# Differential attention on one Trainium2 core: the short tile's row maximum as one reduction and one small scaling

## The chip, the cores and the metric

The kernel runs on one core of a Trainium2 chip. The metric is the device time of one launch in microseconds (us), the median of several runs. A core has a matrix engine (TensorE, PE in the rows, with its weight loads as PEld), a vector engine (VectorE, DVE), an activation engine (ScalarE, ACT), a general engine (GpSimd, POOL) and SyncE (SP), which here issues the transfers. Each has its own instruction stream, and they order one another with semaphores. SBUF is the memory on the chip, PSUM the one into which TensorE writes.

## The reference

The input is x of 8 x 512 x 512 in float32. The output is a chain of three residual blocks, each on a layer-normalised x:

```python
x = x + 0.5 * ffn(layernorm(x))     # expert choice over 16 experts, one shared expert matrix
x = x + attn(layernorm(x))          # differential attention
x = x + 0.5 * ffn(layernorm(x))
```

The attention has 16 heads of width 32 with two maps each and 4 key/value heads. What the change touches is the first softmax, over energies that are masked causally:

```python
energy = where(causal, NEG, einsum("bqhad,bkhad->bahqk", qd, kd))
scores = softmax(energy / sqrt(D), axis=-1)          # a = 0, 1: two maps
diff   = softmax(where(causal, NEG, scores[:, 0] - lam * scores[:, 1]), axis=-1)
att    = einsum("bhqv,bvhd->bqhd", diff, v)          # then an RMS norm per head and @ Wo
```

## The kernel before, in words

The program has three stages: the first FFN, the attention with the first half of the second FFN, and the selection of experts and the last sum. The change lies in the second, from about 350 to 1725 us of the profile.

That stage is a software pipeline. 4096 rows are 32 tiles of 128. A body (`run_bodies`) works on three tiles at once: the attention of tile group K, the preparation of a later tile (layer norm, QKV product, rotary embedding, transposes) and the closing of an earlier one (head norm, output product, residual, second layer norm, router and expert product). Each body has 8 steps j of 3 slots. A step is one pair of query tiles of one head, chosen so that the work is the same in each: `tiles(j)` is (0, 3) for even j and (1, 2) for odd j, a short tile of 1 or 2 key blocks of 128 and a long one of 4 or 3. With two maps the short tile has 2 x 128 or 2 x 256 columns, the long one 2 x 512 or 2 x 384.

All engines run the same 24 slots in the same order, written out by hand in their own lists, each with lags in steps. In one step, for the pair in work:

- TensorE (`energies`, L1559 and L1561) makes the energies of the long tile and then the short one in PSUM and adds the mask.
- VectorE (`row_bias`, L1134) takes one instruction per tile and map: it multiplies the energies in PSUM in place by minus the scale (`nesc`) and accumulates their minimum in `nbias`. An accumulating instruction shows as two in the trace, the main one and a `READ_ACCUMULATOR`.
- ScalarE (`exps`, L1415) computes exp(-1 * value + nbias) from PSUM into `ex`, and accumulates the row sum in `esum`. For the short tile it waits for all four bias values of the step.
- VectorE one step later takes reciprocals (`inv_sums`, L1141) and the factor `gam` (`gamma`, L1148). GpSimd masks (`mask`, L1307) and scales the second map (`scale`, L1314). VectorE subtracts the maps and accumulates the maximum (`difference`, L1160) and makes `dbias` (L1169). GpSimd (`shift`, L1321) and ScalarE (L1424) apply the second softmax's bias, TensorE transposes (`turn_diff`, L1573), ScalarE takes the exponential (`probs`, L1432), and TensorE multiplies by the values (`weigh`, L1591).

Around the attention, in the same order: VectorE's rotary products (L1224, L1233), which GpSimd adds (L1346) and splits (L1361); VectorE's layer-norm statistics (L1195 to L1199); its head sums (L1243 to L1250), from which GpSimd takes a power (`head_root`, L1390); VectorE's head norm (`head_norm`, L1256), whose result goes over ScalarE (L1469) and GpSimd (`low_heads`, L1367) to a transpose on TensorE (L1605); and GpSimd's further work on tiles of 512 columns (`low`, L1352; `square`, L1384). Each engine works in order, so what waits holds up all behind it.

Of the kernel before, what the change touches and what calls it, by code (L numbers as in the profile page):

```python
# [15 lines left out]
ALU = mybir.AluOpType  # L16
# [4 lines left out]
I32 = mybir.dt.int32  # L21
X = mybir.AxisListType.X
# [3 lines left out]
P = 128  # L26
# [38 lines left out]
SC_E, SC_R, SC_Q, SC_O = range(4)  # L65
# [79 lines left out]
def run_bodies(eng, attention, side, ahead, alone, spread, closing):  # L145

    def body(K, tau, pi, pairs=True, more=True):
        known = {}
        for j in range(STEPS):
            for i in range(3):
                for lag, f in attention[i] if pairs else ():  # L160
                    back = j < lag
                    if not isinstance(K, int) or 0 <= K - back < NT:
                        f(Place(known, K, back, (j - lag) % STEPS, j - lag))
                for f in side.get(3 * j + i, ()):
                    f(tau, pi)
                for f in ahead.get(3 * j + i, ()):
                    if tau is not None and more:
                        f(tau + 1)

    for slot in sorted(ahead):  # L170
        for f in ahead[slot]:
            f(0)
    spread[0] = True
    with eng.Fori(0, AHEAD) as tau:
        for f, next_tile in alone:
            f(tau + 1 if next_tile else tau)
    spread[0] = False
    body(0, AHEAD, None)
    with eng.Fori(1, BEHIND) as K:
        body(K, K + AHEAD, None)  # L180
    with eng.Fori(BEHIND, NT - AHEAD - 1) as K:
        body(K, K + AHEAD, K - BEHIND)
    body(NT - AHEAD - 1, NT - 1, NT - 1 - AHEAD - BEHIND, more=False)
    with eng.Fori(NT - AHEAD, NT) as K:
        body(K, None, K - BEHIND)
    body(NT, None, NT - BEHIND)
    spread[1] = True
    for f, next_tile in closing:
        if next_tile:
            f(NT - BEHIND + 1)  # L190
    with eng.Fori(NT - BEHIND + 1, NT - 1) as pi:
        for f, next_tile in closing:
            f(pi + 1 if next_tile else pi)
    for f, next_tile in closing:
        if not next_tile:
            f(NT - 1)
    spread[1] = False


def program(nc, x, wqkv, wo, we, wr, lams, rms, rb, eb, consts, out, x1_d, x2_d, y2_d):  # L200
    top = ExitStack()

    def maker(ctx):
        def sb(name, shape, dt=F32):
            return ctx.enter_context(nc.sbuf_tensor(name, shape, dt))

        def ps(name, shape, dt=F32):
            return ctx.enter_context(nc.psum_tensor(name, shape, dt))

        def sem(name):  # L210
            return ctx.enter_context(nc.semaphore(name))

        return sb, ps, sem

    with top:
# [10 lines left out]
        esc = sb("esc", [P, 4])  # L226
        nesc = sb("nesc", [P, 1])
# [216 lines left out]
        with ExitStack() as ctx:  # L444
# [12 lines left out]
            part = sb1("part", [P, 2, KT])  # L457
# [16 lines left out]
            def spare(first, tiles):  # L474
# [18 lines left out]
            consts_done, bn_done, mv_done, ve_done, nm_done = (sem1(n) for n in (  # L493
                "consts_done", "bn_done", "mv_done", "ve_done", "nm_done"))
            rstd_done, xn_done, xt_done, hi_done, lo_done = (sem1(n) for n in (
                "rstd_done", "a_xn_done", "a_xt_done", "a_hi_done", "a_lo_done"))
# [40 lines left out]
            def _(sp):  # L537
# [30 lines left out]
                for i in range(PIECES):  # L568
                    if i >= 2:
                        sp.wait_ge(piece_lo, i - 1)  # L570
                    source, raw, _, _, _ = piece(i)
                    sp.dma_start(raw, source).then_inc(piece_in[i % 2], 16)
# [352 lines left out]
        with ExitStack() as ctx:  # L925
            sb2, ps2, sem2 = maker(ctx)
# [21 lines left out]
            pr = [sb2(f"pr{i}", [P, PAIR]) for i in range(2)]  # L948

            nbias = sb2("nbias", [P, 8, 2, 2])  # L950
            esum = sb2("esum", [P, 8, 2, 2])
            rsum = sb2("rsum", [P, 8, 2, 2])
            gam = sb2("gam", [P, 8, 2])
# [5 lines left out]
            at = sb2("at", [P, 2, E], F16)  # L959
# [19 lines left out]
            def sig(name, credit=CREDIT):  # L979
                return Signal(sem2(name), credit)  # L980


            x_in, st_done, ve_done, rstd_done, xn_done = sem2("x_in"), sig("st_done"), sig("ve_done"), sig(
                "rstd_done"), sig("xn_done")
            hi_done, lo_done, xt_done, xt_out = sig("hi_done"), sig("lo_done"), sig("xt_done"), sig("xt_out")
            rhi_done, rlo_done = sig("rhi_done"), sig("rlo_done")
            proj_done, rope_v, rope_done, v_done = sig("proj_done"), sig("rope_v"), sig("rope_done"), sig("v_done")
# [2 lines left out]
            ones_set = sem2("ones_set")  # L990

            e_done, bias_done, exp_done = sig("e_done"), sig("bias_done"), sig("exp_done")
            rs_done, gam_done, masked, scaled = sig("rs_done"), sig("gam_done"), sig("masked"), sig("scaled")
            diff_done, dbias_done = sig("diff_done"), sig("dbias_done")
            shifted_short, shifted_long = sig("shifted_short"), sig("shifted_long")
            dt_done, prob_done, av_done, att_out = sig("dt_done"), sig("prob_done"), sig("av_done", 64), sig("att_out")
# [5 lines left out]
            xr_in, st2_done, ve2_done, rstd2_done, xn2_done = sem2("xr_in"), sig("st2_done"), sig("ve2_done"), sig(  # L1002
                "rstd2_done"), sig("xn2_done")
# [25 lines left out]
            def tiles(j):  # L1029

                return ((0, 3), (1, 2))[j % 2]

            def span(j, i):

                first = P * (tiles(j)[0] + 1)
                return (0, first) if i == 0 else (first, PAIR)

            def energy(j, i):


                n = P * (tiles(j)[i] + 1)
                short, long = ((2, slice(0, 2)), (1, slice(0, 4, 3)), (0, slice(2, 4)), (3, slice(1, 3)))[j % 4]
                if i == 0:
                    return bank[:, short, 0:2 * n].rearrange("p (a n) -> p a n", a=2)
                return bank[:, long, 0:n]
# [73 lines left out]

            @blk.vector  # L1120
            def _(dve):
                for s in (st_done, ve_done, xn_done, st2_done, ve2_done, xn2_done, rope_v, bias_done, rs_done, gam_done, diff_done, dbias_done, att_out,
                          ss_done, s2_done, de_done, an_done, x2_done, lg_out):
                    s.start(dve)
                dve.memset(vs[:, :, :, D:DV], 1.0).then_inc(ones_set, 1)


                def row_bias(i):
                    def f(at):
                        j = at.j  # L1130
                        e_done.wait(dve, at.units(2, 1 - i))
                        for a in range(2):
                            part = energy(j, i)[:, a, :]
                            dve.tensor_scalar(part, part, nesc[:, 0:1], None, ALU.mult, ALU.min,  # L1134
                                              accum_out=nbias[:, j, i, a:a + 1]).then_inc(bias_done.sem, 1)
                    return f

                def inv_sums(at):
                    j = at.j
# [12 lines left out]
                def difference(i):  # L1152

                    def f(at):
                        j = at.j
                        if i == 0:
                            scaled.wait(dve, at.units(2, 1))
                            dt_done.wait(dve, at.units(2, 1 - 8), apart_v)
                        lo, hi = span(j, i)
                        dve.tensor_tensor_reduce(out=df[j % 4][:, lo:hi], in0=ex[j % 4][:, 0, lo:hi],  # L1160
                                                 in1=ex[j % 4][:, 1, lo:hi], scale=1.0, scalar=-3e38,
                                                 op0=ALU.subtract, op1=ALU.max, accum_out=dmax[:, j, i:i + 1])\
                           .then_inc(diff_done.sem, 1)
                    return f
# [115 lines left out]
                def take_logits(u):  # L1280
# [2 lines left out]
                       .then_inc(lg_out.sem, 1)  # L1283

                run_bodies(dve,
                           [[(0, row_bias(1)), (0, row_bias(0))],
                            [(1, inv_sums), (1, gamma), (4, diff_bias), (3, difference(0))],
                            [(8, take_head), (3, difference(1))]],
                           {2: [post(head_sums)], 4: [post(head_norm)], 5: [rope(0)], 9: [rope(1)], 11: [post(add)],
# [113 lines left out]
            def _(ac):  # L1403
                for s in (hi_done, xt_out, rhi_done, v_done, turned_out, exp_done, shifted_long, prob_done, ah_done, at_out, hi2_done,
                          xt2_out, y_out):
                    s.start(ac)
                ac.wait_ge(ones_set, 1)

                def exps(i):
                    def f(at):  # L1410
                        j = at.j
                        lo, hi = span(j, i)
                        for a in range(2):
                            bias_done.wait(ac, at.units(4, a if i == 1 else 3))
                            ac.activation(ex[j % 4][:, a, lo:hi], energy(j, i)[:, a, :], ACT.Exp,  # L1415
                                          bias=nbias[:, j, i, a:a + 1], scale=-1.0,
                                          accum_out=esum[:, j, i, a:a + 1]).then_inc(exp_done.sem, 1)
                    return f

# [373 lines left out]
```

## Time and profile before

| | |
|---|---|
| median of 3 runs | 1957.39 us (1941.44 to 1961.42) |
| profiled execution | 1944.41 us, of which the span is 1942.3 us |
| PE, DVE, ACT, POOL busy, share of the span | 77%, 75%, 65%, 56% |
| mean granted TensorE clock | 0.848 of full speed |
| `exps`, ACT L1415 | 1024 instructions, 527.7 us busy |
| `row_bias`, DVE L1134 | 1024 instructions, 503.6 us busy |

How to read it: a busy time is the sum over an engine's instructions, and on VectorE an instruction's record can overlap the next one's, so the distance from start to start tells what an instruction costs its engine. An instruction that the engine has taken up and that waits for a memory port counts as busy. The 1942.3 us hold three stages with different limits; the rows below are mostly of the middle stage.

### The profile page before, as it was taken

Reading aid. Unit: us, or ns where it says so; the run is one execution under the profiler, and the core shown is the slowest. Engines: PE = TensorE matmul, PEld = TensorE weight load, DVE = VectorE, ACT = ScalarE, POOL = GpSimd, SP = SyncE. Lnnn points to the kernel's source line nnn. Section 1 sums busy time; section 2 is a strip of 40 time slices with the busy share of each in tenths; the row PEclk is TensorE's granted clock in tenths of the full one; section 3 lists DMA queues with packets and bytes.
Section 4 is the critical chain, followed back from the end, with each engine's and each line's share of the span. In section 5 each row is a group of like instructions: output and inputs, shape, how many; then the busy total and the mean of one; then the engine's idle time right before and its main releaser. Section 6 shows DMA issues by size and latency. Waiting matters only on the chain. (4 is left out here: it accounts for less than half of the span.)

```text
span 1942.3 us, 44349 instructions
## 1 busy us (share of the span) xinstructions
PE 1497.7 (77%) x10688; PEld 1038.7 (53%) x10688; DVE 1449.4 (75%) x5497; ACT 1258.2 (65%) x3422; POOL 1097.1 (56%) x1505
## 2 busy tenths in 40 slices
PE   3995434588888888998889988998889888885520
PEld 3542211366666666666666666666666666663210
DVE  6687211687889889898898889898898867751268
ACT  2361121687878888888888888887888877852120
POOL 5320222565677777677776777677777655652200
PEclk9997767688889989899999989899999778766655
DMA  7025111111111111121111111121111100001176
GB/s 288 3 81 184 31 35 42 26 38 33 28 32 54 42 42 47 46 53 45 44 53 42 47 42 47 46 53 44 44 53 41 40 16 22 16 17 33 38 268 259
DMA packets 179669, 117.25 MB, mean 60 GB/s; under 512 B 139169, under 2 KB 139553, under 8 KB 179618
## 3 DMA queue, kind: packets, MB, share of 16 engines
q1 hardware_dynamic: 179618, 116.65, 20.4%
q8 instruction: 22, 0.36, 0.1%
q14 instruction: 29, 0.24, 0.0%
HBM read 51.57 MB, written 33.55 MB: 44 GB/s over the span
## 5 line engine op out<-in xcount | busy, mean ns | idle before, releaser
L1415 ACT ACTIVATE ex<-bank,nbias 128x512 f32<-128x512 f32 (+3 forms) x1024 | 527.7, 538 | 67.5 <-DVE bank L1134 64.8
L1134 DVE TENSOR_SCALAR_CACHE_REDUCE bank<-bank,nesc 128x512 f32<-128x512 f32 (+3 forms) x1024 | 503.6, 553 | 61.9 <-PE bank L1561 60.8
L1591 PEld LDWEIGHTS bank<-vs,pr 128*128 128x128 f32 x2560 | 334.6, 206 | 23.2 <-issue 12.2
L1591 PE MATMUL bank<-vs,pr 128*128 (+1 forms) x2560 | 339.7, 284 | 8.6 <-issue 4.1
L1573 PE MATMUL bank<-cst,df 128*128 128x128 f32 x1280 | 264.5, 309 | 86.7 <-ACT pr L1432 85.9
L1314 POOL TENSOR_SCALAR ex<-ex,gam 128x128 f32<-128x128 f32 (+3 forms) x512 | 314.0, 624 | 0.0
L1559 PE MATMUL bank<-ks,qs 96*128 (+2 forms) x1024 | 262.1, 333 | 50.9 <-ACT ex L1415 48.7
L1432 ACT ACTIVATE pr<-bank 128x128 f32<-128x128 f32 (+3 forms) x512 | 231.7, 453 | 88.8 <-PE bank L1573 87.7
L1160 DVE CUSTOM_DVE_ANT_0 df<-ex 128x128 f32<-128x128 f32 (+3 forms) x512 | 258.9, 520 | 8.8 <-issue 4.5
L1573 PEld LDWEIGHTS bank<-cst,df 128*128 128x128 f32 x1280 | 168.0, 165 | 114.2 <-ACT pr L1432 98.3
L1415 ACT ACTIVATION_READ_ACCUMULATOR ex<-bank,nbias 128x1 f32 x1024 | 222.8, 218 | 0.0
L1561 PE MATMUL bank<-mask_b,ident_b 128*128 128x128 bf16 x1024 | 207.7, 237 | 0.0
L1424 ACT ACTIVATE df<-df,dbias,rsum 128x512 f32<-128x512 f32 (+1 forms) x256 | 201.6, 787 | 0.0
L1559 PEld LDWEIGHTS bank<-ks,qs 96*128 (+1 forms) x1024 | 109.7, 107 | 140.9 <-issue 73.3
L1346 POOL TENSOR_TENSOR rot<-rot,scratch 128x512 f32<-128x512 f32 (+1 forms) x96 | 105.1, 1095 | 123.8 <-DVE scratch L1233 123.8
L1321 POOL TENSOR_SCALAR df<-df,rsum,dbias 128x128 f32<-128x128 f32 (+1 forms) x256 | 149.9, 586 | 39.4 <-DVE dbias L1169 39.3
L1361 POOL TENSOR_TENSOR split<-rot,split 128x512 f16<-128x512 f32 (+1 forms) x96 | 95.3, 992 | 123.5 <-ACT split L1460 123.5
L247 PE MATMUL bank<-wqkv_h,b_xt 128*128 128x512 f16 (+1 forms) x384 | 156.2, 407 | 8.0 <-ACT b_xt L1484 5.9
L248 PE MATMUL bank<-wqkv_l,b_xt 128*128 128x512 f16 (+1 forms) x384 | 156.1, 406 | 0.0
L249 PE MATMUL bank<-wqkv_h,b_xt 128*128 128x512 f16 (+1 forms) x384 | 155.7, 406 | 0.0
L1134 DVE DVE_READ_ACCUMULATOR bank<-bank,nesc 128x1 f32 x1024 | 142.9, 140 | 0.0
L1148 DVE SCALAR_TENSOR_TENSOR gam<-esum,lam,rsum 128x2 f32<-128x2 f32 x256 | 115.2, 450 | 33.8 <-DVE rsum L1141 24.9
(279 smaller groups left out, 2958.5 us busy)
## 6 DMA issues: line engine op xcount, KB each, us to landing
qs<-turned SPq DMA_DIRECT2D x384, 64.0 KB, 2.1
x_dram<-xa SPq DMA_DIRECT2D x8, 1024.0 KB, 4.9
b_xs<-x_dram SPq DMA_DIRECT2D x32, 256.0 KB, 2.6
x<-x_dram SPq DMA_DIRECT2D x32, 256.0 KB, 2.6
x_dram<-x SPq DMA_DIRECT2D x32, 256.0 KB, 2.0
y_dram<-scratch SPq DMA_DIRECT2D x32, 256.0 KB, 2.0
c_x<-x_dram SPq DMA_DIRECT2D x8, 1024.0 KB, 14.5
c_y<-y_dram SPq DMA_DIRECT2D x8, 1024.0 KB, 15.0
```

The lines of the kernel that those rows point to most:

```text
L247: eng.matmul(acc, a_hi(k), b_hi(k), start=first and k == 0, stop=False)
L248: eng.matmul(acc, a_hi(k), b_lo(k), start=False, stop=False)
L1134: dve.tensor_scalar(part, part, nesc[:, 0:1], None, ALU.mult, ALU.min, accum_out=nbias[:, j, i, a:a + 1]).then_inc(bias_done.sem, 1)
L1160: dve.tensor_tensor_reduce(out=df[j % 4][:, lo:hi], in0=ex[j % 4][:, 0, lo:hi], in1=ex[j % 4][:, 1, lo:hi], scale=1.0, scalar=-3e38, op0=A ...
L1314: gp.tensor_scalar(ex[j % 4][:, 1, lo:hi], ex[j % 4][:, 1, lo:hi], gam[:, j, i:i + 1], 1.0, ALU.mult, ALU.mult).then_inc(scaled.sem, 1)
L1415: ac.activation(ex[j % 4][:, a, lo:hi], energy(j, i)[:, a, :], ACT.Exp, bias=nbias[:, j, i, a:a + 1], scale=-1.0, accum_out=esum[:, j, i, ...
L1424: ac.activation(df[j % 4][:, lo:hi], df[j % 4][:, lo:hi], ACT.Identity, bias=dbias[:, j, 1:2], scale=rsum[:, j, 1, 0:1]).then_inc(shifted_ ...
L1432: ac.activation(pr[j % 2][:, lo:hi], bank[:, 6, 0:hi - lo], ACT.Exp).then_inc(prob_done.sem, 1)
L1559: pe.matmul(out_e, q.rearrange("p a n -> p (a n)"), k.rearrange("p a n -> p (a n)"), start=True, stop=True)
L1561: mm = pe.matmul(out_e[:, n - P:n], ident_b[:, :], mask_b[:, :], start=False, stop=True, skip_group_check=True)
L1573: tr = pe.transpose(bank[:, 6, k * P:(k + 1) * P], df[j % 4][:, lo + k * P:lo + (k + 1) * P], ident)
L1591: mm = pe.matmul(bank[:, 7, t * DV:(t + 1) * DV], pr[j % 2][:, lo + k * P:lo + (k + 1) * P], val, start=(k == 0), stop=(k == t))
```

## The change

- In VectorE's step, `row_bias(1)` becomes `long_bias`, which is unchanged for the long tile. `row_bias(0)` becomes two functions. `short_max` is one reduction (`tensor_reduce`, maximum) over both maps of the short tile in PSUM, which writes a 128 x 2 tile `smax` and leaves the energies as they are. `short_bias` waits for it on a new semaphore and multiplies `smax` by `nesc` into `nbias`, one `tensor_scalar` of 128 x 2 from SBUF to SBUF.
- ScalarE's short exponentials read unscaled energies, so their scale is the positive one. It is loaded once into a register of ScalarE and given as the instruction's scale in place of the constant -1.
- `bias_done` counts three per step in place of four: two long, one short.

```diff
-                def row_bias(i):
-                    def f(at):
-                        j = at.j
-                        e_done.wait(dve, at.units(2, 1 - i))
-                        for a in range(2):
-                            part = energy(j, i)[:, a, :]
-                            dve.tensor_scalar(part, part, nesc[:, 0:1], None, ALU.mult, ALU.min,
-                                              accum_out=nbias[:, j, i, a:a + 1]).then_inc(bias_done.sem, 1)
-                    return f
+                def long_bias(at):
+                    j = at.j
+                    e_done.wait(dve, at.units(2))
+                    for a in range(2):
+                        part = energy(j, 1)[:, a, :]
+                        dve.tensor_scalar(part, part, nesc[:, 0:1], None, ALU.mult, ALU.min,
+                                          accum_out=nbias[:, j, 1, a:a + 1]).then_inc(bias_done.sem, 1)
+
+                def short_max(at):
+                    e_done.wait(dve, at.units(2, 1))
+                    dve.tensor_reduce(smax[:, at.j, :], energy(at.j, 0), X, ALU.max).then_inc(smax_done.sem, 1)
+
+                def short_bias(at):
+                    smax_done.wait(dve, at.units(1))
+                    dve.tensor_scalar(nbias[:, at.j, 0, :], smax[:, at.j, :], nesc[:, 0:1], None, ALU.mult)\
+                       .then_inc(bias_done.sem, 1)
...
-                           [[(0, row_bias(1)), (0, row_bias(0))],
+                           [[(0, long_bias), (0, short_max), (0, short_bias)],
...
+                reg = ac.alloc_register("energy_scale")
+                ac.reg_load(reg, esc[0:1, SC_Q:SC_Q + 1].bitcast(I32))
...
-                            bias_done.wait(ac, at.units(4, a if i == 1 else 3))
+                            bias_done.wait(ac, at.units(3, a if i == 1 else 2))
                             ac.activation(ex[j % 4][:, a, lo:hi], energy(j, i)[:, a, :], ACT.Exp,
-                                          bias=nbias[:, j, i, a:a + 1], scale=-1.0,
+                                          bias=nbias[:, j, i, a:a + 1], scale=-1.0 if i == 1 else reg,
```

## Rows read from the trace of the kernel before

**Rows 1.** Engines' busy time by stretch: length, PE, PEld, DVE, ACT, POOL, granted clock, DMA, GB/s
```profile
900.00:1100.00 200.00, 179.71 (x1390) 129.61 (x1389) 179.98 (x704) 167.39 (x470) 150.50 (x210) 0.94 0.18 47
...
1019.00:1022.00 3.00, 3.00 (x11) 1.43 (x11) 2.20 (x13) 3.00 (x12) 0.60 (x1) 0.50 0.00 0
```

**Rows 2.** Waits from 500 to 1500 us: who for whom, total us, times, longest
```profile
DVE bank L1134 <- PE bank L1561: 35.7, 25, 2.5
DVE att L1180 <- PE bank L1591: 20.1, 17, 2.2
...
ACT ex L1415 <- DVE bank L1134: 36.4, 29, 1.8
...
PE bank L1605 <- POOL split L1367: 17.8, 21, 1.2
```

**Rows 3.** Timeline of VectorE, two steps: start, length, instruction, idle time before it
```profile
1000.49 0.49 DVE L1134 TENSOR_SCALAR_CACHE_REDUCE bank<-bank,nesc 128x256 f32<-128x256 f32 x1
...
1000.89 0.18 DVE L1141 RECIPROCAL rsum<-esum 128x4 f32<-128x4 f32 x1
1001.31 0.22 DVE L1148 SCALAR_TENSOR_TENSOR gam<-esum,lam,rsum 128x2 f32<-128x2 f32 x1 [0.24 <-DVE rsum L1141]
...
1006.85 0.35 DVE L1134 TENSOR_SCALAR_CACHE_REDUCE bank<-bank,nesc 128x128 f32<-128x128 f32 x1
...
1007.12 0.17 DVE L1141 RECIPROCAL rsum<-esum 128x4 f32<-128x4 f32 x1
1007.33 0.54 DVE L1148 SCALAR_TENSOR_TENSOR gam<-esum,lam,rsum 128x2 f32<-128x2 f32 x1
1007.79 1.32 DVE L1169 SCALAR_TENSOR_TENSOR dbias<-dmax,rsum 128x2 f32<-128x2 f32 x1
```

**Rows 4.** Groups of instructions, whole trace: busy us, mean ns, idle before
```profile
L1243 DVE TENSOR_REDUCE ast<-scratch 128x16 f32<-128x512 f32 x28 | 19.1, 680 | 0.9 <-POOL scratch L1384 0.9
...
L649 DVE TENSOR_REDUCE most<-cb 2x1 f32<-2x128 f32 x2 | 0.5, 260 | 0.0
```

**Rows 5.** Timeline of VectorE: layer-norm statistics, each waiting for the one before
```profile
1030.13 0.68 DVE L1195 BATCH_NORM_STATS2 norms<-b_xs 128x6 f32<-128x512 f32 x1
1030.97 0.18 DVE L1197 BATCH_NORM_AGGREGATE norms<-norms 128x2 f32<-128x6 f32 x1 [0.15 <-DVE norms L1195]
1031.18 0.15 DVE L1199 TENSOR_SCALAR norms<-norms 128x1 f32<-128x1 f32 x1
1031.28 0.18 DVE L1141 RECIPROCAL rsum<-esum 128x4 f32<-128x4 f32 x1
```

**Rows 6.** Timelines of VectorE and GpSimd in the first stage, one moment
```profile
117.15 1.39 DVE L349 TENSOR_SCALAR a_step<-a_step 128x3 int32<-128x3 int32 x1
...
116.99 1.52 POOL L774 TENSOR_TENSOR wqkv_l<-a_xn,wqkv_h 128x704 f16<-128x704 f32 x1 [27.45 <-ACT wqkv_h L820]
```

**Rows 7.** Timeline of GpSimd over one body
```profile
999.21 2.92 POOL L1390 TENSOR_TENSOR ast<-ast,half 128x16 f32<-128x16 f32 x1 [2.05 <-DVE ast L1250]
...
1006.83 1.03 POOL L1314 TENSOR_SCALAR ex<-ex,gam 128x128 f32<-128x128 f32 x2
1007.84 1.26 POOL L1346 TENSOR_TENSOR rot<-rot,scratch 128x512 f32<-128x512 f32 x1
...
1011.53 0.41 POOL L1307 TENSOR_SCALAR_AFFINE_SELECT ex<-ex 128x256 f32<-128x256 f32 x1
...
1034.94 1.15 POOL L1352 TENSOR_TENSOR split<-b_xs,split 128x512 f16<-128x512 f32 x1
...
1040.87 1.04 POOL L1384 TENSOR_TENSOR scratch<-att 128x512 f32 x1 [1.38 <-DMA y_dram<-scratch]
1044.84 2.92 POOL L1390 TENSOR_TENSOR ast<-ast,half 128x16 f32<-128x16 f32 x1 [2.93 <-DVE ast L1250]
```

**Rows 8.** Groups by shape from 400 to 1500 us: busy us, mean ns, idle before
```profile
L1148 DVE SCALAR_TENSOR_TENSOR gam<-esum,lam,rsum 128x2 f32<-128x2 f32 x202 | 100.2, 496 | 27.2 <-DVE rsum L1141 19.3
```

More of the change, by code:

```diff
@@ L950, in program @@
             nbias = sb2("nbias", [P, 8, 2, 2])
+            smax = sb2("smax", [P, 8, 2])
             esum = sb2("esum", [P, 8, 2, 2])
@@ L992, in program @@
             e_done, bias_done, exp_done = sig("e_done"), sig("bias_done"), sig("exp_done")
+            smax_done = sig("smax_done")
             rs_done, gam_done, masked, scaled = sig("rs_done"), sig("gam_done"), sig("masked"), sig("scaled")
@@ L1121, in _ @@
             def _(dve):
-                for s in (st_done, ve_done, xn_done, st2_done, ve2_done, xn2_done, rope_v, bias_done, rs_done, gam_done, diff_done, dbias_done, att_out,
+                for s in (st_done, ve_done, xn_done, st2_done, ve2_done, xn2_done, rope_v, bias_done, smax_done, rs_done, gam_done, diff_done, dbias_done, att_out,
                           ss_done, s2_done, de_done, an_done, x2_done, lg_out):
```

## The prediction

> **What bounds the kernel now.** I read the page first, then busy time by stretch, then who waits for whom, then the timelines of VectorE and GpSimd through one body. In the middle stage three engines are nearly full: in 200 us TensorE is busy 179.7, VectorE 180.0 and ScalarE 167.4 us, GpSimd 150.5 [rows 1]. So no engine alone sets the pace. The waits say how the load is passed on. From 500 to 1500 us VectorE waits for TensorE's energies 25 times, 35.7 us, and for the weighted values 17 times, 20.1 us [rows 2]. A body takes 45.6 us, the distance of two GpSimd powers at 999.21 and 1044.84 [rows 7], so the 1000 us hold 22 bodies, and VectorE has (35.7 + 20.1) / 22 = 2.5 us of real slack in each, mostly in two pieces, behind TensorE's large products. In the other direction ScalarE waits for VectorE's biases 29 times, 36.4 us or 1.65 us a body, and TensorE waits once in nearly each body (21 times) for GpSimd's L1367 [rows 2], the end of a chain from VectorE's head sums over GpSimd's power, VectorE's head norm and GpSimd again. On these two paths a late VectorE makes others late.
>
> **The stream that is removed.** Per step the change takes away the short tile's two L1134 with their accumulator reads. Start to start the 128-column one costs 1007.12 - 1006.85 = 0.27 us, the 256-column one 1000.89 - 1000.49 = 0.40 us [rows 3]. So 0.54 us go in an even step, 0.80 us in an odd one.
>
> **The reduction.** It runs over the same elements, 256 or 512. The nearest rows: a reduction of 128 columns from PSUM takes 0.260 us, one of 512 from SBUF 0.680 us [rows 4], which is 1.09 ns an element between them. Hence 0.40 us for 256 elements and 0.68 us for 512. A wide one from PSUM has no row, so I take the line through these two; were it to cost what the removed pair does, 0.54 and 0.80 us, it would lie 0.13 us higher, and that is its other bound.
>
> **The scaling and its wait.** `short_bias` reads what the instruction in front of it writes. The statistics show what that costs: L1197 starts 0.84 us after a L1195 of 0.68 us, 0.16 us behind its end, and after a short one, L1197 of 0.18 us, L1199 starts 0.21 us later, 0.03 us behind its end [rows 5]. The reduction is like the former, so 0.16 us, with 0.03 as the lower bound. The next instruction starts 0.10 us after a small dependent one (1031.18 to 1031.28) [rows 5]. Even step: 0.40 + 0.16 + 0.10 = 0.66 us for 0.54; odd step: 0.68 + 0.16 + 0.10 = 0.94 us for 0.80. VectorE loses 0.13 us a step, 1.0 us a body; with 0.03 for the wait it is nothing, with the dearer reduction 0.26 us. Four instructions for two save nothing here, since the removed ones were already overlapped and the new pair is not.
>
> **What the scaling meets.** The decisive term is elsewhere. In the first stage a `tensor_scalar` of only 128 x 3, SBUF to SBUF, starts at 117.15 and takes 1.39 us, to 118.54; GpSimd's L774 runs from 116.99 to 118.51 [rows 6]. It ends when GpSimd's instruction does. The same shows in the attention on two-input instructions: `gam` at 1007.33 ends at 1007.87, as the two L1314 of 1.03 us from 1006.83 do, and `dbias` ends at 1009.11, with L1346 (1007.84 plus 1.26) [rows 3, 7]. The L1134 that go never show it, since they work in PSUM. `short_bias` is a multi-column SBUF `tensor_scalar` like L349, so it should wait for whatever GpSimd has in hand. I placed it in the eight steps of the body, just ahead of the end of the short L1134: at 1000.8, 1007.05, 1011.7, 1019.4, 1025.1, 1030.05, 1035.1 and 1041.8 us. GpSimd is idle at three of them. Left to run are 0.3 us of the first L1314 (it ends half way, at 1007.35), 0.25 us of L1307 (to 1011.94), 1.0 us of L1352 (to 1036.09) and 0.1 us of L1384 (to 1041.91) [rows 7]. At 1000.8 the power L1390 runs until 1002.13, yet `gam` inside it, at 1001.31, takes its plain 0.22 us [rows 3, 7], so I count nothing there. The sum is 1.65 us a body, 0.21 us a step. An upper check: `gam`, some tenths later in the same steps, takes 0.496 us in the mean against 0.22 undisturbed, 0.28 us a step [rows 3, 8]. Zero is the lower bound, if the new instruction slips in between.
>
> The Trainium skill says the same of the port (SBUF — State Buffer, "Who interferes with whom"): VectorE and GpSimd share a pair of ports as an exclusive lock, a `tensor_scalar` without accumulator from SBUF can run in the two-port mode that needs it, a `tensor_reduce` never does. The trace agrees for L349's 1.39 us. The page speaks against this change: the one instruction it adds is of the kind that contends, those it removes are not.
>
> **ScalarE.** The two short exponentials keep their shape. [...] ScalarE does the two long exponentials first, so the short bias mostly has cover; without it, a wait at L1352 as at 1035.1 would hold it up by up to 1.0 us.
>
> **The sum.** VectorE gets 1.0 + 1.65 = 2.7 us a body against 2.5 us of slack. If it spread perfectly nearly all would vanish. It doesn't: the slack lies at two places, and hand-overs in between come late. What passes, per body: (a) the step ahead of the head sums is on the chain to TensorE's L1605, with 0.13 us and L1384's 0.1 us, 0.23; (b) ScalarE waits for a bias 29 times in 22 bodies, 1.3 a body, and each of these is late by a step's 0.13 + 0.21 us, of which I let half be given back at ScalarE's other idle time, 0.22; (c) GpSimd in turn stands behind `short_bias` for about its own 0.15 us (L1199) [rows 5] in some steps, 0.15. Together 0.6 us a body, by 32 bodies 19 us. The profiled 1944.4 would become 1963.6 us, 1.0% more. It was a fast one of its kind, 13 us under the median of 1957.4, so against the median I predict 1977 us.
>
> **The rivals.**
> - *All is absorbed.* The port wait takes only what `gam` behind it would have waited for the same GpSimd instruction, as at 1035.1, and the two slacks of 2.5 us take the rest. VectorE's waits for L1561 and L1180 shrink instead. For it: the sum is hardly over the slack. Against: TensorE's 21 waits at the end of VectorE's chain. Time: plus 0 to 6 us, 1957 to 1963.
> - *The power holds the port as well.* L1390 stretches `short_bias` from 1000.8 to 1002.13, 1.3 us; then `gam`, `dbias`, a subtraction and only then the head norm, which now starts 0.2 us behind the power's end: some 0.7 us later, on the chain to L1605, in the 27 bodies that have one, 19 us on top: 1996 us. For it: L349 waits for the whole of L774. Against: `gam` isn't touched inside L1390, though it has two inputs rather than one. The skill's page has it so that GpSimd keeps the pair for the whole instruction.
> - *The clock falls further.* At 1019 to 1022 us the granted clock is 0.50, the 1.2 GHz level [rows 1], right after TensorE had waited for ScalarE. Over 200 us it is 0.94, so 12% of the time is at that level. If TensorE's longer waits add one such stretch of 3 us a body, 1.5 us each or 33 to 48 us are lost: about 2000 us.
> - *Faster, by the same clock.* The pattern of waits repeats in each body, so a shift of some tenths can also take TensorE's wait ahead of one slow stretch away. A 3 us stretch at full clock gives 1.5 us a body back, less the 0.6 above: minus 0.9 by 32, 29 us, 1928 us. It decides from where this wait falls away in most bodies. For it: the wait before it is on ScalarE, whose order of short exponentials moves. Against: every term on VectorE is a delay.
>
> **How the numbers follow.** Forecast, 0.5% to 2% slower: 0.42. Absorbed: 0.25. Power: 0.11. Clock, slower: 0.08. Faster: 0.14. About 1% is what a measurement of this kernel can tell from no change. Slower by over 1% gets half of the forecast and nearly all of the power and clock cases, 0.21 + 0.10 + 0.08 plus a share for the port wait at its bound of 0.28 a step, 0.06: 0.45. Faster by over 1%: 0.12. The rest, 0.43, is within 1%. The range takes in absorbed and power and leaves out most of the faster and the clock case: 1943 to 2004 us. The forecast's own range is 1967 to 1996.
>
> **What would show it.** In the profile after: two groups for the short tile, a reduction of about 0.40 and 0.68 us and a `tensor_scalar` 128x2 of 0.15 us undisturbed but 0.3 to 0.4 us in the mean, with single ones of 1 us that end with GpSimd's L1352. If its mean is 0.15 to 0.2, the port step is wrong. If its longest are 1.3 us and more inside L1390, the power holds the port. VectorE's waits for L1561 and L1591 should shrink from 35.7 and 20.1 us if it absorbs; ScalarE's wait for biases should grow over 36.4 us. The start-to-start distance of reduction and scaling tests the 0.16 us. The exponentials' mean tests the register. The granted clock in the middle stage, 0.94, tests the clock rivals. The prediction is wrong as a whole if the body becomes shorter than 45.6 us.

## The result, and the profile after

| | before | after |
|---|---|---|
| median of 20 runs each | 1941.23 us | 1964.66 us |
| ratio, 95% interval | | 1.0106 (1.0084 to 1.0129) |
| profiled execution, its span | 1944.41 us, 1942.3 us | 1963.25 us, 1961.5 us |
| mean granted clock of TensorE | 0.848 | 0.835 |

The changed kernel is 1.1% slower. The three runs of before that the prediction had to go by, 1941 to 1961 us, lay high; over twenty the median is 1941. So the 1.0% was met and the 1977 us is 12 us too high for that reason; 1964.7 us lies within the range of 1943 to 2004 and just under the forecast's own band of 1967 to 1996. The twenty runs of before form two groups, fifteen at 1937 to 1946 us and five at 1957 to 1966, while the changed kernel's twenty all lie at 1962 to 1967. A second batch gave 1.0079 (1.0047 to 1.0110) for the same pair, with the kernel before at 1955 us and the changed one at 1964; the loss is about 1%.

The short tile's new instructions, groups by shape from 400 to 1500 us (busy us, mean ns, idle before), beside [rows 8]:

```profile
L1157 DVE SCALAR_TENSOR_TENSOR gam<-esum,lam,rsum 128x2 f32<-128x2 f32 x199 | 88.5, 445 | 27.2 <-DVE rsum L1150 19.0
L1144 DVE TENSOR_SCALAR nbias<-smax,nesc 128x2 f32<-128x2 f32 x199 | 72.1, 362 | 7.1
...
L1140 DVE TENSOR_REDUCE smax<-bank 128x2 f32<-128x512 f32 x99 | 67.6, 683 | 0.0
...
L1140 DVE TENSOR_REDUCE smax<-bank 128x2 f32<-128x256 f32 x100 | 41.6, 416 | 0.0
```

The reductions take the 0.42 and 0.68 us that two rows of before had given. The scaling has a mean of 0.362 us; over the whole trace its shortest and median are 0.227 and 0.229 us and its longest 1.117. 77 of the 256 are stretched, to 0.65 us in the mean; the rest take their plain 0.23. The timeline of VectorE shows one of each kind:

```profile
1000.27 0.41 DVE L1140 TENSOR_REDUCE smax<-bank 128x2 f32<-128x256 f32 x1
1000.72 0.23 DVE L1144 TENSOR_SCALAR nbias<-smax,nesc 128x2 f32<-128x2 f32 x1
1000.86 0.69 DVE L1204 BATCH_NORM_STATS2 norms<-b_xs 128x6 f32<-128x512 f32 x1
...
1005.06 0.68 DVE L1140 TENSOR_REDUCE smax<-bank 128x2 f32<-128x512 f32 x1
1005.78 1.06 DVE L1144 TENSOR_SCALAR nbias<-smax,nesc 128x2 f32<-128x2 f32 x1
1006.75 0.16 DVE L1150 RECIPROCAL rsum<-esum 128x4 f32<-128x4 f32 x1
...
1014.86 0.69 DVE L1140 TENSOR_REDUCE smax<-bank 128x2 f32<-128x512 f32 x1
1015.59 0.23 DVE L1144 TENSOR_SCALAR nbias<-smax,nesc 128x2 f32<-128x2 f32 x1
1015.72 0.17 DVE L1150 RECIPROCAL rsum<-esum 128x4 f32<-128x4 f32 x1
```

And what GpSimd does at the second and the third of them:

```profile
1005.66 1.15 POOL L1361 TENSOR_TENSOR split<-b_xs,split 128x512 f16<-128x512 f32 x1
...
1013.98 2.92 POOL L1399 TENSOR_TENSOR ast<-ast,half 128x16 f32<-128x16 f32 x1 [2.04 <-DVE ast L1259]
```

L1144 at 1005.78 ends at 1006.84, GpSimd's L1361 (L1352 of before) at 1006.81: the predicted wait for the port, at the predicted place. The one at 1015.59 lies wholly inside GpSimd's power and takes its plain 0.23 us, as do all 27 that lie inside a power in this trace: the power does not hold the port against it. Start to start, reduction and scaling cost 0.59 us in an even step (1000.27 to 1000.86) and 0.86 in an odd one (1014.86 to 1015.72), against 0.54 and 0.80 us before [rows 3].

Waits from 500 to 1500 us, of VectorE for TensorE and of ScalarE for VectorE, beside [rows 2]:

```profile
DVE bank L1135 <- PE bank L1572: 38.3, 25, 2.3
...
DVE att L1189 <- PE bank L1602: 7.7, 12, 1.7
```

```profile
ACT ex L1426 <- DVE bank L1135: 37.5, 28, 1.8
...
ACT ex L1426 <- DVE nbias L1144: 10.6, 25, 0.4
```

VectorE's slack at the weighted values shrinks from 20.1 to 7.7 us, so part of the load is absorbed there; its waits for the energies, 35.7 us before, stay. ScalarE waits for the short bias 25 times. Before, its 29 waits in these 1000 us were all at the long tile's exponentials.

**Where the time went.** GpSimd's power comes once in each body with closing work. The first starts at 561.45 us in the trace before and at 571.11 in the one after, the 21st at 1436.10 and at 1457.04. Of the 19.2 us between the two spans, 9.7 us have come by the first power (0.8 of them before the attention's first L1134, at 351.95 and 352.78). The next 20 bodies take 874.65 us before and 885.93 after, 0.56 us more a body. What follows is 1.7 us shorter after. So the first five bodies lose 1.8 us each and the next 20 a third of that, though every body got the same eight reductions and scalings.

The 20 bodies aren't all 0.56 us longer, either. Five of them before and three after, from power to power (columns as in [rows 1], the length first, the granted clock third from the end):

```profile
868.74:912.98 44.24, 40.05 (x305) 28.72 (x304) 39.08 (x154) 36.53 (x104) 32.35 (x45) 0.92 0.18 47
912.98:957.12 44.14, 39.57 (x302) 28.40 (x301) 38.92 (x154) 36.35 (x103) 32.37 (x46) 0.92 0.18 45
957.12:999.21 42.09, 37.35 (x306) 27.28 (x305) 39.66 (x154) 36.71 (x104) 32.35 (x46) 1.00 0.19 49
999.21:1044.84 45.63, 41.01 (x300) 28.93 (x301) 39.13 (x154) 36.17 (x103) 31.95 (x46) 0.89 0.17 44
1044.84:1087.16 42.32, 37.82 (x301) 27.72 (x301) 39.04 (x154) 36.15 (x103) 32.45 (x45) 0.96 0.18 47
```

```profile
924.68:969.73 45.05, 40.44 (x304) 28.81 (x303) 40.44 (x138) 37.20 (x104) 32.42 (x45) 0.92 0.18 47
969.73:1013.98 44.25, 39.70 (x301) 28.39 (x301) 40.04 (x138) 36.07 (x103) 32.40 (x45) 0.92 0.17 44
1013.98:1058.23 44.25, 39.85 (x304) 28.50 (x303) 40.04 (x138) 36.56 (x103) 32.40 (x45) 0.92 0.18 46
```

A body's length goes with its clock. Before, ten of the 20 have 0.92 and 44.22 us in the mean, four 1.00 and 42.1, three 0.96 and 42.3 to 42.6, three 0.89 and 45.6. After, sixteen have 0.92 and 44.33 in the mean, one 1.00, one 0.96, and two 0.89 and 0.90. At the same clock the changed kernel's body is 0.1 us longer. The other 0.45 us a body is the mix: the bodies with little or no time at the lower level are nearly gone. A second trace of the changed kernel, from the batch below, has 886.00 us for its 20 bodies. In the first bodies the clock differs as well. Busy time from 350 to 560 us, before and then after:

```profile
350.00:560.00 210.00, 172.75 (x1158) 123.74 (x1159) 169.93 (x707) 161.62 (x479) 127.77 (x195) 0.83 0.14 32
```

```profile
350.00:560.00 210.00, 176.51 (x1112) 125.16 (x1112) 164.29 (x599) 155.49 (x457) 119.48 (x183) 0.77 0.14 30
```

The granted clock falls from 0.83 to 0.77. One place holds 2.6 us of the loss. TensorE's timeline before has the weighted values of one step and the last product of a projection at

```profile
435.60 1.20 PE L1591 MATMUL bank<-vs,pr 128*128 x10
...
439.26 0.38 PE L249 MATMUL bank<-wqkv_h,b_xt 128*128 128x512 f16 x1
```

and after at

```profile
438.03 2.18 PE L1602 MATMUL bank<-vs,pr 128*128 x10
...
444.34 0.38 PE L249 MATMUL bank<-wqkv_h,b_xt 128*128 128x512 f16 x1
```

The same work takes 3.7 us from start to start before, 6.3 us after. From 437 to 444 us TensorE is busy all the time in both, though not on the same work throughout, with these clocks, before and after:

```profile
437.00:444.00 7.00, 7.00 (x46) 4.17 (x44) 5.56 (x24) 4.68 (x16) 3.73 (x5) 1.00 0.24 51
```

```profile
437.00:444.00 7.00, 7.00 (x29) 4.71 (x28) 3.35 (x14) 4.23 (x13) 2.63 (x5) 0.54 0.34 73
```

46 matmuls at the 2.4 GHz level against 29, nearly all at 1.2 GHz. Both traces have the lower level before this; TensorE had waited in both for ScalarE 1.5 us some ten us earlier. It was at 0.50 from about 430 us on in both, until about 435 us before and 443 after. Why it stayed down longer these rows don't tell, nor why the later bodies settle at 0.92.

### The profile page after: what moved, and what is told of

The parts are those of the page before. It is cut to its first block and busy times, and to the rows that moved or that the text cites. A ratio compares the mean times of both kernels' runs of the same rounds, so it can differ in the third digit from the quotient of the medians.

```text
span 1961.5 us, 43869 instructions
## 1 busy us (share of the span) xinstructions
PE 1522.2 (78%) x10688; PEld 1052.1 (54%) x10688; DVE 1474.3 (75%) x4985; ACT 1263.0 (64%) x3422; POOL 1098.6 (56%) x1505
## 5 line engine op out<-in xcount | busy, mean ns | idle before, releaser
L1135 DVE TENSOR_SCALAR_CACHE_REDUCE bank<-bank,nesc 128x512 f32<-128x512 f32 (+1 forms) x512 | 330.4, 685 | 64.0 <-PE bank L1572 63.1
L1570 PE MATMUL bank<-ks,qs 96*128 (+2 forms) x1024 | 268.7, 339 | 47.0 <-ACT ex L1426 44.6
L1169 DVE CUSTOM_DVE_ANT_0 df<-ex 128x128 f32<-128x128 f32 (+3 forms) x512 | 274.7, 551 | 7.1 <-issue 2.6
L1426 ACT ACTIVATION_READ_ACCUMULATOR ex<-bank,nbias 128x1 f32 x1024 | 216.4, 211 | 0.0
L1572 PE MATMUL bank<-mask_b,ident_b 128*128 128x128 bf16 x1024 | 211.5, 240 | 0.0
L247 PE MATMUL bank<-wqkv_h,b_xt 128*128 128x512 f16 (+1 forms) x384 | 159.5, 415 | 8.0 <-ACT b_xt L1495 5.9
L249 PE MATMUL bank<-wqkv_h,b_xt 128*128 128x512 f16 (+1 forms) x384 | 160.0, 417 | 0.0
L1140 DVE TENSOR_REDUCE smax<-bank 128x2 f32<-128x256 f32 (+1 forms) x256 | 140.8, 550 | 0.0
L1616 PE MATMUL bank<-ident_h,split 128*128 128x128 f16 x768 | 70.4, 245 | 88.8 <-POOL split L1361 34.3
```

Of the source, the lines that this page charges most:

```text
L249: mm = eng.matmul(acc, a_lo(k), b_hi(k), start=False, stop=last and k == KT - 1)
L1570: pe.matmul(out_e, q.rearrange("p a n -> p (a n)"), k.rearrange("p a n -> p (a n)"), start=True, stop=True)
L1572: mm = pe.matmul(out_e[:, n - P:n], ident_b[:, :], mask_b[:, :], start=False, stop=True, skip_group_check=True)
```

## The experiments

Theory A is the prediction's: VectorE loses time to the stream (the exposed scaling) and to the port, and others wait for it. Theory B: what counts is any load on VectorE, the port wait being one load among others. Theory C: TensorE's clock sets the size of the loss. All ratios are to the kernel before on the same chip. The median of the kernel before differs between the batches, from 1941 to 1955 us, while the changed kernel gave 1964.7 and 1964.1 us in its two; where two runs of different batches are set side by side in microseconds, this should be kept in mind.

**Two narrow scalings for the wide one.** In the changed kernel:

```diff
-dve.tensor_scalar(nbias[:, at.j, 0, :], smax[:, at.j, :], nesc[:, 0:1], None, ALU.mult)\
-   .then_inc(bias_done.sem, 1)
+for a in range(2):
+    ins = dve.tensor_scalar(nbias[:, at.j, 0, a:a + 1], smax[:, at.j, a:a + 1], nesc[:, 0:1], None, ALU.mult)
+ins.then_inc(bias_done.sem, 1)
```

> The changed kernel with its one scaling of 128x2 split into two of 128x1, one per map; all else is as in the changed kernel. Port theory: the scaling of 128x2 lost 133 ns a step in the mean (362 measured, 229 undisturbed) waiting for GpSimd's instruction. If only an instruction of several columns can take the second port, the two narrow ones stay at their undisturbed length of 0.15 to 0.23 us with nothing over 0.3, VectorE gains the port wait and pays one more instruction of about 0.1 us a step, and the time comes down from 1964.7 towards 1950 to 1958 us. Rival, the pair itself: the loss is the exposed scaling and its wait, so an extra instruction makes it worse, 1965 to 1975 us, even if the port wait is gone. Rival, the clock: the time moves by 5 to 20 us either way with the granted clock and not with VectorE's load.

Measured: 1961.16 us, ratio 1.0060 (1.0041 to 1.0078). The group by shape, from 400 to 1500 us:

```profile
L1145 DVE TENSOR_SCALAR nbias<-smax,nesc 128x1 f32<-128x1 f32 x398 | 66.6, 209 | 7.1
```

All 512 of them took 0.202 to 0.216 us. None of these 128x1 instructions waited for GpSimd; of the 128x2 ones 77 in 256 did. But the time came down by only some 3 us from the changed kernel's 1964.7, short of the 1950 to 1958 us that the port theory expected, so the port wait of 0.13 us a step is not the main part, or the additional instruction (0.11 us a step) took most of the gain.

**An unused scaling in the kernel before.** The same two widths, where nobody waits for them:

```diff
+def spare(at):
+    dve.tensor_scalar(spare_b[:, at.j, 0:2], spare_a[:, 0:2], nesc[:, 0:1], None, ALU.mult)
...
-[[(0, row_bias(1)), (0, row_bias(0))],
+[[(0, row_bias(1)), (0, row_bias(0)), (0, spare)],
```

> The kernel before with one unused scaling of 128x2, SBUF to SBUF, behind the short tile's two minimum instructions in every step. Nobody waits for it, and no wait stands before it. Port theory: it takes 0.36 us in the mean, is stretched to the end of GpSimd's instruction as in the changed kernel, and the kernel takes about as long as the changed one or somewhat more, 1.0% to 1.6% over before. Rival, absorbed: VectorE's slack takes it, under 0.3% over before, and the changed kernel's loss then comes from another part.

> As the kernel with the unused scaling of 128x2, but the spare instruction is 128x1. It costs VectorE the same undisturbed 0.14 us start to start. Port theory: no record is stretched and the time is within 0.5% of before; the difference between the two spare kernels is the port wait alone, 0.5% to 1%. If it is as slow as the one with two columns, the load on VectorE is what costs, not the port. If a 128x1 instruction is stretched too, the port is wanted at any width.

Measured: 1962.90 us, ratio 1.0068 (1.0047 to 1.0089) with 128x2, and 1961.39 us, 1.0058 (1.0038 to 1.0079) with 128x1. Their groups, the wide and then the narrow:

```profile
L1141 DVE TENSOR_SCALAR spare_b<-spare_a,nesc 128x2 f32<-128x2 f32 x199 | 73.6, 370 | 0.0
```

```profile
L1141 DVE TENSOR_SCALAR spare_b<-spare_a,nesc 128x1 f32<-128x1 f32 x198 | 40.7, 205 | 0.0
```

The port wait shows in the records, 370 against 205 ns, and hardly in the time: 1.5 us, within the intervals. The load does: one narrow instruction of 0.13 us start to start, 33 us over 256 steps, for which nobody waits, costs 11 us. Both results miss the port theory, which had 1.0% to 1.6% for the first and under 0.5% for the second.

**The register.** Before, with the short exponentials' scale of -1 from a register.

> The kernel before with the short tile's exponentials taking their scale, still -1, from a register of ScalarE in place of the constant; nothing else changes. All theories that I hold: no difference, ratio 0.997 to 1.003, and the exponentials' mean stays at 538 ns. If it is 0.5% slower or more, the register's scale is part of the loss.

Measured: 1951.44 us, ratio 1.0003 (0.9987 to 1.0019). A scale from a register costs nothing that this interval can show.

**The changed kernel again, the same load twice, and the gap covered.** One batch on one chip.

> The changed kernel as it is, beside the others on one chip, so that their ratios can be compared. Ratio 1.008 to 1.013, as measured first. The spare kernels gave 1.0058 with 0.13 us of load a step and 1.0068 with the port wait on top. If this one is at 1.010 again though its load is only 0.06 us and its port wait 0.13 us a step, the rest must come from somebody who waits for the scaling: ScalarE, with 25 waits of 10.6 us for it.

> The kernel before with two unused scalings of 128x1 a step in place of one, 0.25 us of load a step. If the loss is in proportion to the load, 1.1% to 1.2% over before. If slack absorbs the first part, more than double, over 1.5%. If what counts is a threshold or the clock, it stays near the 0.6% of the single one.

Measured: the changed kernel 1964.12 us, 1.0079 (1.0047 to 1.0110); two narrow spare instructions 1964.26 us, the same ratio and interval. Twice the load costs 3 us more than once, not 11 more. A loss in proportion to the load would be 1.1% to 1.2%, at the upper end of the interval or over it, so it is unlikely. Whether the changed kernel loses something of its own because ScalarE waits for it, as the first expectation argues for a ratio of 1.010, stays open: its 0.19 us a step of load and port wait cost what 0.25 us of pure load cost.

The other two move the reciprocal of the step before ahead, so that its distance to `gam` is filled. In the kernel before:

```diff
-[[(0, row_bias(1)), (0, row_bias(0))],
- [(1, inv_sums), (1, gamma), (4, diff_bias), (3, difference(0))],
+[[(0, row_bias(1)), (1, inv_sums), (0, row_bias(0))],
+ [(1, gamma), (4, diff_bias), (3, difference(0))],
```

and in the changed kernel between `short_max` and `short_bias`.

> The kernel before with only the reciprocal moved ahead of the short tile's two minimum instructions, so that the wait between reciprocal and gam is covered. VectorE's load falls by about 0.15 to 0.2 us a step. Load theory: the mirror of the spare instruction, 0.3% to 0.8% faster than before. Rival, absorbed: VectorE's slack is only made larger, no change within 0.3%. A risk is that the reciprocal waits for the row sums one instruction earlier; then waits of VectorE for ScalarE's L1415 appear.

> The changed kernel with the reciprocal of the step before moved between the reduction and the scaling. The scaling no longer stands directly behind the reduction, and it fills the gap of 0.15 to 0.32 us that stood between the reciprocal and gam. VectorE gains about 0.15 us a step, the port wait stays at 0.13 us. Load theory (0.13 us a step cost 0.58%): the ratio to before falls by 0.4 to 0.7 points, to about 1.004. Port theory: it stays above 1.008, since the port wait is as it was. If the body's length hangs on the clock only, either sign is possible.

Measured: 1916.62 us, ratio 0.9839 (0.9779 to 0.9898), from the kernel before; 1930.11 us, 0.9886 (0.9852 to 0.9920), from the changed one. The first is the fastest kernel of this study. The second misses both of its expectations, about 1.004 and over 1.008, on the fast side. VectorE's timeline in the first:

```profile
1009.55 0.18 DVE L1141 RECIPROCAL rsum<-esum 128x4 f32<-128x4 f32 x1
1009.64 0.33 DVE L1134 TENSOR_SCALAR_CACHE_REDUCE bank<-bank,nesc 128x128 f32<-128x128 f32 x1
...
1009.89 0.36 DVE L1134 TENSOR_SCALAR_CACHE_REDUCE bank<-bank,nesc 128x128 f32<-128x128 f32 x1
...
1010.16 0.22 DVE L1148 SCALAR_TENSOR_TENSOR gam<-esum,lam,rsum 128x2 f32<-128x2 f32 x1
```

`gam` follows without a gap, where the step of [rows 3] at 1000.89 had 0.24 us of idle time. The groups of `gam` in the two kernels, from 400 to 1500 us, first from before, then from the changed one:

```profile
L1148 DVE SCALAR_TENSOR_TENSOR gam<-esum,lam,rsum 128x2 f32<-128x2 f32 x207 | 88.1, 426 | 0.0
```

```profile
L1157 DVE SCALAR_TENSOR_TENSOR gam<-esum,lam,rsum 128x2 f32<-128x2 f32 x205 | 79.1, 386 | 2.5 <-issue 0.2
```

No wait for the reciprocal is left in either [rows 8]. With the gaps covered the change still costs 13.5 us, 0.7%, between these two. The expectation of the load theory, 0.3% to 0.8% faster, was too small: it is 1.6% (1.0% to 2.2%). Two bodies of the kernel with the early reciprocal, from power to power, show a part of the reason:

```profile
1031.45:1075.08 43.63, 38.84 (x296) 27.80 (x296) 38.70 (x154) 35.77 (x102) 32.74 (x46) 0.92 0.17 46
1075.08:1116.79 41.71, 37.52 (x310) 27.60 (x309) 39.47 (x154) 36.73 (x105) 32.68 (x46) 1.00 0.20 50
```

At either clock a body is 0.4 to 0.6 us shorter than before (44.22 and 42.1), and from here on every second body has 1.00 where before it was one in five. The 20 bodies take 859.07 us against 874.65, so about a third of the gain is the mix again.

**Where the load counts.** The narrow spare instruction in part of the bodies only:

> The unused scaling of 128x1 only in the first five bodies of the attention, 40 steps, where no closing work runs. With it in all 32 bodies the time was 1961.4 us, 0.58% over before, and in the changed kernel half of the loss, 9.7 us, had come by the end of these bodies. Load theory, even: 40 of 256 steps give 0.09%, 2 us. Clock theory: the stretches at the lower level in these bodies grow as they did (54.6 us before, some 74 to 84 with the load), and the time rises by 5 to 10 us, 0.3% to 0.5%.

> The unused scaling of 128x1 only in the 21 bodies in which all three tiles are at work, 168 steps. Load theory, even: 0.38%, 7.5 us. Clock theory with the first bodies: 0.1% to 0.3%, the complement of what the kernel with the load in the first five bodies shows.

Measured: in the first five bodies, 40 steps, 1954.12 us, ratio 1.0038 (1.0017 to 1.0060); in the 22 bodies in which all three tiles are at work, 176 steps (the expectation's 21 and 168 leave one out), 1951.99 us, 1.0029 (1.0012 to 1.0046). Less than a quarter of the steps of the second costs about as much; the intervals overlap. The 40 instructions are 5 us of load and the loss is about 7 us, what the clock theory had (0.3% to 0.5%) and the even load theory had not (0.09%). The second lies between its two expectations. The stretch of the first bodies with the load in them:

```profile
350.00:560.00 210.00, 175.73 (x1112) 123.78 (x1110) 164.77 (x712) 153.16 (x454) 117.64 (x181) 0.78 0.13 30
```

The clock is 0.78, as with 0.77 in the changed kernel, against 0.83 before; in the kernel with the load in the full bodies it is 0.83 there again. These are single traces, so the others count: with load behind the short tile in these bodies, seven traces have 0.76 to 0.79 there; without any, three have 0.81 to 0.83 (0.81 is the register kernel, with ratio 1.0003). So a small load on VectorE behind the short tile goes with the lower clock in these bodies, with neither the port nor the scaling's semaphore in play. It need not show at the place at 437 us: the kernel with the 128x2 spare instruction has 1.00 there and 0.78 over the stretch.

**Another place, and on top of the better kernel.**

> The unused scaling of 128x1 in all bodies, but at the end of VectorE's step, behind the second subtraction, in place of behind the short tile's minimum. The load is the same 0.13 us a step; what it delays directly is the next step's work and not gam. Load theory: 0.4% to 0.7% over before, as at the other place. If the place is what matters, because gam and with it GpSimd's chain come late, under 0.3%.

> The kernel with the reciprocal moved ahead (1916.6 us) plus the unused scaling of 128x1 behind the short tile's minimum. If the move gained because it took 0.15 to 0.3 us of load from VectorE, the spare instruction of 0.13 us gives about half of that back: 1928 to 1940 us. If it gained because it made slack that now absorbs a small load, under 1922 us.

Measured: at the end of VectorE's step 1963.78 us, ratio 1.0091 (1.0073 to 1.0109), more than at the first place and than the 0.4% to 0.7% expected. So it isn't `gam` coming late. Its trace has 0.80 from 350 to 560 us. Counted from the attention's first minimum, its first power comes only 2.0 us later than before (211.5 and 209.5 us), with the load in the first five bodies alone 11.1 us later (220.6). Its loss comes in the bodies behind that, 20 of which take 887.1 us. On top of the moved reciprocal 1933.84 us, ratio 0.9942 (0.9925 to 0.9958), 17 us over the kernel without it in the other batch and within the 1928 to 1940 us expected if the move had taken load away: 0.13 us a step costs about 0.9% there, with an uncertainty of half a percent or more from the other kernel's interval. VectorE's waits in that faster kernel without the spare instruction, 500 to 1500 us:

```profile
DVE bank L1134 <- PE bank L1561: 34.2, 25, 2.7
DVE att L1180 <- PE bank L1591: 28.0, 23, 3.4
DVE an L1256 <- POOL ast L1390: 19.4, 22, 0.9
```

It has more idle time than before on two of the three (20.1 us for L1591 in [rows 2]), and a small load still isn't absorbed. Idle time in the sum is not slack.

**The clock over runs of one kernel.** The three batches hold 66 runs of the kernel before, two of 1968 and 1971 us left out. The 17 with a granted clock of 0.847 or more have a median of 1942.0 us, the 12 with 0.840 or less one of 1957.3 us. One hundredth of clock goes with 17 us, in a program whose instructions are the same. The changed kernel's 20 runs lie at 0.832 to 0.839 and 1962 to 1967 us, on the same line: against the medians of the 66, 0.845 and 1948 us, it takes 0.011 less clock and 17 us more. The kernels with spare load lie somewhat above the line (medians of 0.838 and 1964 us with two spare instructions, where the line gives about 1959), so there part of the loss is plain delay. A line through runs doesn't say which is cause and which effect. The single place at 437 us, the same matmuls at half speed, shows that the lower level itself costs time, and the bodies of equal clock, of nearly equal length before and after, show that little of the changed kernel's loss is anything else. What isn't shown is how a load on VectorE brings the lower level about.

So theory B is right that a load costs time though nobody waits for it, and that the port wait is a small part. Theory C is right on where the time goes. Of theory A the delays are seen in the rows, but they aren't what the time was lost to in the main.

## Why the prediction was right

- *The stream that is removed and the reduction.* 0.54 and 0.80 us, and 0.42 and 0.68 us: as predicted. The line through a narrow reduction from PSUM and a wide one from SBUF held for a wide one from PSUM.
- *The scaling's wait.* Mis-sized. I took 0.16 us from the statistics instruction; it is 0.04 us (1000.27 plus 0.41 to 1000.72), near the lower bound of 0.03 that I had from a short instruction. The next instruction starts 0.14 us later and not 0.10; the scaling itself takes 0.23 us and not 0.15. The stream's loss is 0.05 and 0.06 us a step in place of 0.12 and 0.14.
- *The port.* The mechanism was right, in place and in kind, and the narrow scalings, none of which is stretched, bear it out from the other side. The size was 0.21 us a step, measured are 0.362 less 0.229, 0.13 us. The wait of a stretched one was right, 0.41 us in the mean predicted and 0.42 measured; there are fewer of them, three in ten and not four in eight. The Trainium skill's rule on the shared pair (SBUF — State Buffer, "Who interferes with whom") agrees for `tensor_scalar`, 1.06 us, and for `tensor_reduce`, never stretched over 0.690 us. Where the Trainium skill says there that whoever issues first has the pair for its whole instruction, the trace differs for the power: 0.23 us inside one of 2.92 us.
- *ScalarE.* The forecast's sum has no term for the register, and its kernel shows none, ratio 1.0003; its waits for biases grew from 36.4 to 48.1 us in 1000, in the direction of term (b).
- *The sum.* The range and the ratio were right, the account of how the time is lost was not. 2.7 us a body of load was predicted and 1.5 us came (0.06 plus 0.13, by eight). 0.6 us a body was predicted to pass as plain delay, and 19 us came, 0.6 by 32. That agreement is luck in the main. The step that failed is the one that passes the load on as an even delay: between bodies of the same clock the changed kernel loses 0.1 us, 3 to 4 us over 32 bodies. The rest came with TensorE's clock: 0.45 us a body in the 20 full ones, and in the first five, which have no closing work, the clock fell from 0.83 to 0.77 and 1.8 us a body were lost. The slack of 2.5 us a body was read from the full bodies and applied to all.
- *The body.* The 45.6 us between two powers [rows 7] belong to the longest kind of body, the one at 0.89 in the rows above. The mean is 43.7 us before (874.65 by 20) and 44.3 after, so 1000 us hold 23 bodies, and "wrong as a whole if the body becomes shorter than 45.6 us" measured nothing: bodies were shorter than that already.
- *The rivals.* Absorbed: as a time it is excluded by the interval, though at equal clock it is nearly what the bodies show. The power: excluded by the row. The clock, slower, had 8% and a price of 33 to 48 us: the loss is mostly of this kind, at under half of that price, and the clock should have been part of the forecast, not beside it. That longer waits of TensorE are what brings it isn't shown. Faster: not seen in the changed kernel; by stretches of 200 us from 700 to 1500 us the granted clock is 0.91 to 0.94, against 0.93 to 0.94 before. Its mechanism is seen in the kernel with the early reciprocal, and a body without a slow stretch gives back 2.1 us (44.22 to 42.1), where 1.5 was put.

What stays open: how 1.5 us of load on VectorE leads to more time at TensorE's lower level, around 440 us, where TensorE's waits are nearly the same in both traces, and in the full bodies; why the load at the end of the step loses its time elsewhere; and how much of the changed kernel's 1% is the port. The spare kernels put the port wait at 1.5 us and the narrow scalings at some 3 us, neither of which is clear of the measurement.

## What to carry to other kernels

Where three engines are 84% to 90% busy, price an edit by the load that it puts on the vector engine, start to start, and don't count its idle time as slack: 0.13 us a step cost a third to a half of itself. Before replacing instructions, look for a wait of an engine on its own last result and move an instruction that is ready into it; one line moved gave 1.6% here, more than the whole change was about. Keep a small scaling at one column if GpSimd is busy. Judge a kernel whose clock wavers by many runs, and before a longer body is called a delay, compare bodies with the same granted clock: here they differed by 0.1 us, and the mix made the rest. Take the body's length as a mean over many; neighbours differed by up to 3.5 us.

## What the runs showed of the hardware that I had not expected

- A `tensor_scalar` of 128x1 from SBUF did not wait for GpSimd in any of 512 records (0.202 to 0.216 us), one of 128x2 did in 77 of 256 (up to 1.117 us).
- GpSimd's power on 128x16, 2.92 us, doesn't hold up a 128x2 `tensor_scalar` of VectorE (0.23 us in all 27 inside one).
- A dependent instruction started 0.04 us behind the end of a reduction from PSUM, but 0.16 us behind the statistics instruction [rows 5].
- Runs of one unchanged program spread from 1936 to 1962 us; those with a granted clock of 0.847 or more have a median of 1942 us, those with 0.840 or less one of 1957.
- Bodies of the same instructions within one execution take 42.1, 42.3, 44.2 or 45.6 us, with a granted clock of 1.00, 0.96, 0.92 or 0.89.
